# A folded self-attention product T done in three float32r passes, with new high and low parts of the sums and of the values' weights

## What is computed

```python
x = _layernorm(x + self_attention_without_softmax(x))     # (q k^T) v, 8 heads of 64, then w_o
x = _layernorm(x + cross_attention(x, ctx_1024, mask))    # softmax over 154 keys, 16 heads of 32
x = _layernorm(x + ffn(x))                                # sigmoid(x_r W_r) * (relu(x_k W_k)^2 W_v)
```

```
T   = G Wv' + s bv'            (512x512)
K'V = T' Wk' and a bias term   (only the blocks of one head count)
U   = K'V Wo',   M = Wq' U + 1,   y = x M + c
```

## Time and profile before

| | |
|---|---|
| median of 3 runs | 918.23 us (918.06 to 918.87) |
| the profiled execution | 918.05 us, of which its span, first to last instruction, is 916.3 us |
| TensorE busy | 903.6 us, 99% of the span |
| VectorE busy | 715.3 us, 78% |
| granted TensorE clock | 0.998 of full speed |

### The profile page before, as it was taken

How to read it: one execution, slowest core, us unless ns; L and a number is a source line. 1 busy time by engine, 2 the same in 40 slices (tenths; PEclk the granted TensorE clock), 3 DMA queues, 4 the chain that set the end, 5 groups by cost and what they waited for, 6 DMA issues and landing times.

```text
span 916.3 us, 19065 instructions
## 1 busy us (share of the span) xinstructions
PE 903.6 (99%) x6726; PEld 735.5 (80%) x6726; DVE 715.3 (78%) x1994; ACT 552.3 (60%) x1667; POOL 507.2 (55%) x505
## 2 busy tenths in 40 slices
PE   8999999999999999999999999999999999999997
PEld 7867767777888888887878888888787878787876
DVE  7697566577887878797979788887878787879775
ACT  7455236857765656565757575756665757575631
POOL 1053015858684757575756657575666766656420
PEclk9999999999999999999999999999999999999999
DMA  8771020113010000002000000101010100100001
GB/s 300 240 248 49 27 91 9 35 43 127 9 47 9 30 26 24 31 24 89 24 31 24 31 24 24 31 25 31 24 30 25 31 25 14 41 2 24 2 24 46
DMA packets 31033, 45.65 MB, mean 50 GB/s; under 512 B 2779, under 2 KB 15579, under 8 KB 30811
## 3 DMA queue, kind: packets, MB, share of 16 engines
q1 hardware_dynamic: 27339, 37.36, 12.7%
q10 hardware_dynamic: 3600, 7.08, 2.2%
HBM read 34.10 MB, written 9.70 MB: 48 GB/s over the span
## 4 chain that ended last, share of the span: by engine, by line
PE 75%; DVE 5%; issue 3%; POOL 3%; ACT 1%; POOLq 0%; ACTq 0%
PE dense L88 18%; PE dense L90 17%; PE dense L89 17%; PE turned L1590 5%; PE scores L1578 4%; PE rest_value L1604 4%; PE rest_value L1608 3%; PE dense L1477 2%; PE turned L1477 1%; PE rest_value L1596 1%; POOL row_inv L1383 1%; POOL prob L1389 1%; PE scores L1483 1%; DVE prob L1112 1%; DVE stats L1071 1%
## 5 line engine op out<-in xcount | busy, mean ns | idle before, releaser
L1383 POOL TENSOR_TENSOR row_inv<-row_sum,minus_one 128x4 f32<-128x4 f32 x128 | 145.9, 1139 | 255.1 <-ACT prob L794 253.5
L794 ACT ACTIVATE prob<-prob,row_min 128x154 f32<-128x154 f32 x512 | 209.5, 417 | 17.8 <-DVE row_min L1112 17.8
L1389 POOL TENSOR_TENSOR prob<-prob,row_inv 128x512 f32<-128x512 f32 x128 | 142.1, 1110 | 0.0
L1112 DVE CUSTOM_DVE_ANT_0 prob<-scores,mask_add 128x154 f32<-128x154 f32 x512 | 127.1, 310 | 3.7 <-PE scores L1578 3.7
L802 ACT ACTIVATE prob_t<-turned 128x512 f32<-128x512 f32 x128 | 75.9, 593 | 57.5 <-PE turned L1590 57.4
L794 ACT ACTIVATION_READ_ACCUMULATOR prob<-prob,row_min 128x1 f32 x512 | 98.7, 193 | 0.0
L1590 PE MATMUL turned<-ident,prob 128*128 128x128 f32 x512 | 77.0, 273 | 1.3 <-ACT prob_t L802 0.8
L88 PE MATMUL dense<-xt_hi,cross_wq_hi 128*128 128x256 f32 x256 | 75.0, 293 | 0.5 <-DVE xt_lo L1103 0.5
L88 PE MATMUL dense<-mix_k_hi,ffn_wk_hi 128*128 128x256 f32 x256 | 74.5, 291 | 0.0
L1170 DVE TENSOR_TENSOR k_act_lo<-square,k_act_hi 128x512 fp32r<-128x512 f32 x32 | 50.3, 1573 | 28.2 <-ACT k_act_hi L827 28.2
L89 PE MATMUL dense<-xt_lo,cross_wq_hi 128*128 128x256 f32 x256 | 72.2, 282 | 0.0
(11 more groups left out here) (296 smaller groups left out, 2709.4 us busy)
## 6 DMA issues: line engine op xcount, KB each, us to landing
x_rows<-x_rows SPq DMA_DIRECT2D x32, 256.0 KB, 3.6
xt_raw<-x_cols SPq DMA_DIRECT2D x16, 512.0 KB, 3.7
out<-gate_then_y SPq DMA_DIRECT2D x15, 512.0 KB, 2.8
mask_in<-mask SPq DMA_DIRECT2D x16, 154.0 KB, 2.4
cross_wv<-cross_wv SPq DMA_DIRECT2D x2, 512.0 KB, 5.9
cross_wk<-cross_wk SPq DMA_DIRECT2D x1, 1024.0 KB, 8.7
self_wv<-self_wv ACTq DMA_DIRECT2D x1, 1024.0 KB, 7.6
self_wk<-self_wk ACTq DMA_DIRECT2D x1, 1024.0 KB, 12.0
```

What stands on the lines that cost most here:

```text
L794: m = act.activation(keys, keys, ACT.Exp, bias=row_min[:, buf, t, h:h + 1], scale=-1.0, accum_out=row_sum[:, buf, t, h:h + 1])
L1112: m = dve.tensor_tensor_reduce(prob[buf][:, t, h * CTX:(h + 1) * CTX], s_bank[:, h, t * CTX:(t + 1) * CTX], mask_add[n % 2][:, t, :], -SCA ...
L1383: pool.tensor_tensor(row_inv[:, buf, t, :], row_sum[:, buf, t, :], minus_one[:], ALU.pow).then_inc(*p_inv.up)
L1389: pool.tensor_tensor(keys[:, :, 0:P], keys[:, :, 0:P], inv.broadcast_to([P, HPG, P]), ALU.mult).then_inc(*p_norm.up)
```

## The change

T of both batches is done as three float32r passes. For that:

- G of each batch gets a high part (ScalarE, `sums_high`, four operations of 128x512) and a low part (VectorE, `sums_low`, four).
- The values' weights `self_wv` get a high part (ScalarE, one operation of 128x2048) and a low part (VectorE, one). ScalarE makes the high one after `high(14, 15)` and VectorE the low one before `low(16, 17)`. `self_wv` is put elsewhere in memory, and its load is issued later: after the keys of the context are out, not before them.
- TensorE's order: T's first half now comes after tiles 20 and 21 instead of before, K'V after tiles 24 and 25, U after tile 28; the tiles of x that follow are the same in all.
- In `layers` VectorE builds `s_part` from the high part (four operations, as before from the whole) and then adds the low part's share (four more), after `weight_low("ffn_wk")`.
- At the end of the prologue the adding of 1 to M's diagonal (`add_one`) is split from the low part of M, so that `sums_low(1)` fits between.

```diff
@@ load and high part of the weights, ScalarE
-            load_square("self_wv")
-            load_row("self_bv")
             load_square("self_wk")
...
+            load_square("self_wv")
+            load_row("self_bv")
             high(12, 13)
             load_row("self_bk")
-            high(14, 15, 16, 17)
+            high(14, 15)
+            weight_high("self_wv")
+            high(16, 17)
             take_sums(0)
...
             high(20, 21)
             load_square("self_wq")
+            sums_high(0)
             high(22, 23)
+            def sums_high(b):
+                for i in range(KT):
+                    act.wait_ge(*g_whole.at(b, i + 1))
+                    act.activation(g_two[b][0][:, i, :], g[b][:, i, :], ACT.Copy).then_inc(*g_act.up)
...
                 act.activation(t[0][:, i, :], m_bank[i][:], ACT.Copy).then_inc(*m_out.up)
+                if i == 0:
+                    sums_high(1)
@@ VectorE
-            low(*range(10, 18))
+            low(*range(10, 16))
+            weight_low("self_wv")
+            low(16, 17)
             take_sums(0)
             low(18, 19)
             take_mirror(0)
             low(20, 21)
+            sums_low(0, *range(KT))
             take_columns(0)
+            def sums_low(b, *parts):
+                for i in parts:
+                    dve.wait_ge(*g_act.at(b, KT // 2 + i + 1))
+                    dve.tensor_tensor(g_two[b][1][:, i, :], g[b][:, i, :], f32(g_two[b][0][:, i, :]),
+                                      ALU.subtract).then_inc(*g_whole.up)
...
-            take_m(0)
-            take_m(1)
+            add_one(0)
+            dve.wait_ge(*xt_high.at(0))
+            dve.tensor_tensor(xt_lo[:], xt_in[:], f32(xt_hi[:]), ALU.subtract).then_inc(*xt_low.up)
+            take_m(0)
+            add_one(1)
+            sums_low(1, 0, 1)
+            take_m(1)
+            sums_low(1, 2, 3)
+            add_one(2)
@@ TensorE
-                        m = pe.matmul(t_bank[i][:], g[0][:, k, i * P:(i + 1) * P], f["self_wv"][:, k, :],
-                                      start=(k == 0), stop=(k == KT - 1))
+                        m = three_pass(pe, t_bank[i][:], [x[:, k, i * P:(i + 1) * P] for x in g_two[0]],
+                                       [x[:, k, :] for x in self_wv_two], first=(k == 0), last=(k == KT - 1))
...
             columns(0)
-            pe.wait_ge(*f_here["self_wv"].at(0))
+            sums(20, 21)
+            pe.wait_ge(*w_low.at(place_of("self_wv")))
+            pe.wait_ge(*g_whole.at(0))
             t_product(0, 1)
-            sums(20, 21)
+            sums(22, 23)
             pe.wait_ge(*s_ok.at(0))
             t_product(2, 3)
-            sums(22, 23)
+            sums(24, 25)
...
-            sums(24, 25, 26, 27)
+            sums(26, 27, 28)
...
-            sums(28, 29, 30, 31)
+            sums(29, 30, 31)
@@ layers
-            sum_weights()
+            sum_weights(0)
             take_t(0)
...
                     take_t(2)
                     weight_low("ffn_wk")
+                    sum_weights(1)
...
-                        m = pe.matmul(t1_bank[i], g1[:, k, i * P:(i + 1) * P], fold["self_wv"][:, k, :],
-                                      start=(k == 0), stop=(k == KT - 1))
+                        m = three_pass(pe, t1_bank[i], [x[:, k, i * P:(i + 1) * P] for x in g1_two],
+                                       [x[:, k, :] for x in wv_two], first=(k == 0), last=(k == KT - 1))
```

More of the change, by code:

```diff
@@ L128, in prologue @@
     u0, u0_two, wq_two = f["u"][0], f["u_two"][0], f["wq_two"]
+    g_two, self_wv_two = f["g_two"], f["wv_two"]
     gram = [banks[0:4], banks[4:8]]
@@ L137, in prologue @@
     early = ("cross_wq", "cross_wo")
-    splits = [weights[name] for name in early] + [(f["self_wq"], *wq_two)]
+    splits = {"self_wv": (f["self_wv"], *self_wv_two), **{name: weights[name] for name in early},
+              "self_wq": (f["self_wq"], *wq_two)}
+    place_of = list(splits).index
     t_bank, u_bank, m_bank = ([banks[i] for i in x] for x in ((3, 0, 1, 2), (1, 2, 3, 0), (1, 2, 3, 0)))
@@ L224, in high, with weight_high @@
                     act.activation(x_half[j % RING], by_k(x_in[j % RING]), ACT.Copy, scale=0.5).then_inc(*halved.up)
-            def weight_high(i):
-                raw, hi, _ = splits[i]
-                act.wait_ge(*(w_here[early[i]] if i < len(early) else f_here["self_wq"]).at(0))
+            def weight_high(name):
+                raw, hi, _ = splits[name]
+                act.wait_ge(*(w_here if name in early else f_here)[name].at(0))
                 act.activation(hi[:], raw[:], ACT.Copy).then_inc(*w_high.up)
@@ L273, in act_program @@
             load_square("self_wq")
+            sums_high(0)
             high(22, 23)
             load_row("self_bo")
-            for i in range(len(splits)):
-                weight_high(i)
+            for i, name in enumerate((*early, "self_wq")):
+                weight_high(name)
                 high(2 * i + 24, 2 * i + 25)
@@ L310, in low, with weight_low @@
                     dve.tensor_tensor(by_k(x_lo[i]), by_k(x_in[i]), f32(x_hi[i]), ALU.subtract).then_inc(*split_lo.up)
-            def weight_low(i):
-                raw, hi, lo = splits[i]
-                dve.wait_ge(*w_high.at(i))
+            def weight_low(name):
+                raw, hi, lo = splits[name]
+                dve.wait_ge(*w_high.at(place_of(name)))
                 dve.tensor_tensor(lo[:], raw[:], f32(hi[:]), ALU.subtract).then_inc(*w_low.up)
@@ L370, in dve_program @@
             take_t(0, 1)
-            weight_low(0)
+            weight_low("cross_wq")
             low(24, 25)
-            weight_low(1)
+            weight_low("cross_wo")
             take_t(2, 3)
             low(26, 27)
-            weight_low(2)
+            weight_low("self_wq")
+            low(28)
             dve.wait_ge(*kv_mm.at(0))
@@ L379, in dve_program @@
                 dve.tensor_copy(kv_t[0][r, q, r], kv_bank[r, c]).then_inc(*kv_ok.up)
-            low(28, 29)
-            low(30, 31)
+            low(29, 30, 31)
             def c_times(q, at):
@@ L420, in dve_program @@
             take_m(2)
+            add_one(3)
             take_m(3)
@@ L467, in mirror @@
                 pe.wait_ge(*g_dve.at(b))
-                pe.wait_ge(*g_act.at(b))
+                pe.wait_ge(*g_act.at(b, KT // 2))
                 for i in range(KT):
@@ L474, in columns @@
             def columns(b):
-                pe.wait_ge(*g_whole.at(b))
+                pe.wait_ge(*g_whole.at(b, KT))
                 pe.wait_ge(*summed.at((b + 1) * HALF - 1))
@@ L538, in pe_program @@
                 pe.matmul(u_bank[q][:], kv_t[0][:, q, :], f["self_wo"][:, q, :], start=True, stop=True).then_inc(*u_mm.up)
-            sums(28, 29, 30, 31)
+            sums(29, 30, 31)
             pe.wait_ge(*u_ok.at(0))
             pe.wait_ge(*c_part_ok.at(0, 2 + KT))
-            pe.wait_ge(*w_low.at(2))
+            pe.wait_ge(*w_low.at(place_of("self_wq")))
             m_product(0)
@@ L552, in pe_program @@
             pe.wait_ge(*m_out.at(0, 1))
+            pe.wait_ge(*g_whole.at(1))
             for k in range(KT):
-                pe.matmul(t1_bank[:], g[1][:, k, 0:P], f["self_wv"][:, k, :], start=(k == 0), stop=(k == KT - 1))
+                three_pass(pe, t1_bank[:], [x[:, k, 0:P] for x in g_two[1]], [x[:, k, :] for x in self_wv_two],
+                           first=(k == 0), last=(k == KT - 1))
         with nc.Block():
@@ L598, in layers @@
     col_sb = io["col_sb"]
-    g1, t1, kv_t1, u1 = (fold[x][1] for x in ("g", "t", "kv_t", "u"))
-    u1_two, wq_two = fold["u_two"][1], fold["wq_two"]
+    g1_two, t1, kv_t1, u1 = (fold[x][1] for x in ("g_two", "t", "kv_t", "u"))
+    u1_two, wq_two, wv_two = fold["u_two"][1], fold["wq_two"], fold["wv_two"]
     s_col, s_part, c_part = (fold[x] for x in ("s_col", "s_part", "c_part"))
@@ L1019, in take_t, with sum_weights @@
                                              ALU.mult, ALU.add).then_inc(*ft_ok.up)
-            def sum_weights():
-                dve.tensor_scalar(s_part[:], fold["self_bv"][:], float(S) / P, None, ALU.mult).then_inc(*fs_part.up)
+            def sum_weights(half):
+                if half == 0:
+                    dve.tensor_scalar(s_part[:], fold["self_bv"][:], float(S) / P, None, ALU.mult).then_inc(*fs_part.up)
                 for k in range(KT):
-                    dve.wait_ge(*fs_part.at(0, k + 1))
-                    dve.scalar_tensor_tensor(s_part[:], fold["self_wv"][:, k, :], s_col[:, 1, k:k + 1], s_part[:],
+                    dve.wait_ge(*fs_part.at(0, half * KT + k + 1))
+                    dve.scalar_tensor_tensor(s_part[:], f32(wv_two[half][:, k, :]), s_col[:, 1, k:k + 1], s_part[:],
                                              ALU.mult, ALU.add).then_inc(*fs_part.up)
@@ L1882, in decoder_layer @@
             "g": [mem.over("x1_0", "g0", square), mem.over("mix_k_hi", "g1", square)],
```

(4 more changed lines are left out.)

11 lines of the change are left out of this document (5 added, 6 removed).

## The result

The changed kernel takes **919.89 us** in the median of 15 runs (918.51 to 922.12), the kernel before 918.06 (917.61 to 918.87, 15 runs beside it): a ratio of 1.0020, 95% interval 1.0012 to 1.0028. That is a small loss at the edge of 0.2%, where 917.0 and a small gain were forecast, and outside the range.

The account below looks back on a forecast made before the run. TensorE, busy 99% of the span, was taken as the bound. -5.5 saved + 0.7 (layers' turning) + 0.7 (tile 16) + 2.9 (T) = -1.2 us, so the median 918.23 becomes 917.0 us; range 914.3 to 919.0.

Parts of the forecast that it names:

- What TensorE saves: Eight parts of T in three passes: each takes 2.74 us instead of 3.43, saving 5.5 us in all.
- What of that stands in the layers: Layers keep 1.4 us of 2.1; 0.7 becomes a wait before the turning; the prologue's end gives 0.7.
- about 0.5: Layers, before VectorE's first scores: about 0.5 us of cover left after s_part's added steps; without it up to 0.7 lost.
- Tile 16: Tile 16, ahead of T of batch 0: TensorE waits 0.7 us behind the values' weight's split; bounds 0.7 and 5.6.
- the third rival: Before tile 16: the values' weight lands after 12.0 us, TensorE waits 5.6 us, time 921.9 us; chance 0.07.
- The price of a meeting: Around T of batch 0: a GpSimd add meeting VectorE costs 1.07 us per low part, 0.9 per s_part step.
- their number: Before tile 22's low part: four GpSimd adds meet VectorE's work, the middle of three and five.
- From there to M: From tile 22's low part to M: no further loss counted, bounds 0.5 for VectorE and 0.3 at U.
- the step *T.: T of batch 0: TensorE waits 2.9 us in sum, at T's start or tile 22; bounds 1.8 and 4.0.
- VectorE's queue has no gap: Around T of batch 0: five adds are due and VectorE works without a pause in which they could run unmet.
- Rival 4: Layers' 1.4 us gain is lost too, or six adds meet at T: 918.4 us; chance 0.14 (to 919).

Follow-up runs that it names:

- batch 0 as before: Changed kernel with T of batch 0 back in float32 and its old place, self_wv split behind tile 29; 916.21 us.
- the fastest: Changed kernel with three weights' loads, self_wv's split and s_part later, T's parts 2 and 3 taken ahead of cross_wo's low part; 914.56 us.
- the fill: Changed kernel plus four float32 matmuls that compute nothing, two ahead of tile 21 and two ahead of T; 919.62 us.
- second profile: Changed kernel without further edit, measured again on another chip, median 919.97 us; the profile is of its run of 923.27 us.
- loads later: Changed kernel with the loads of cross_wo, self_wq and self_wo issued behind the high parts of tiles 20 and 21; 916.70 us.
- adds on one column: Changed kernel with GpSimd adding only one column of tiles 20 to 31 into batch 1's column sums, output wrong; 916.99 us.
- both later: Changed kernel with the three weights' loads behind tile 21's copies and self_wv's split behind tiles 16 and 17; 917.78 us.

## Why the prediction was wrong

**Right, by its steps.** *What TensorE saves*: T's second half takes 5.54 us, 74.41 to 79.95, 2.77 a part for 2.74. *What of that stands in the layers*: the turning's wait is 0.65 for 0.7. VectorE's cover before its first scores is 0.66 for "about 0.5", in its timeline:
```profile
133.74 3.11 DVE L1062 SCALAR_TENSOR_TENSOR s_part<-self_wv_lo,s_col,s_part 128x512 f32<-128x512 f32 x4
137.50 0.32 DVE L1149 CUSTOM_DVE_ANT_0 prob<-scores,mask_add 128x154 f32<-128x154 f32 x1 [0.66 <-PE scores L1616]
```
Layers and prologue's end together came out at 2.2 for 2.1, by the experiment with batch 0 as before. *Tile 16*: 0.56 by its bracket and 0.72 by its start, for 0.7; the values' weight took 5.6 us to land, for 6 to 6.5, so the third rival was out. The price of a meeting, 1.07 us, is right, and so is their number: with the tiles in time four meet, and tile 22's low part is taken at 66.67 for 66.8. *From there to M* is right as well: from tile 22 to M it is 28.63 us in the changed kernel (71.37 to 100.00) and in the fastest (64.02 to 92.65), for the 28.6 of the forecast.

**Wrong: the step *T.***, "2.9 us in sum, at T's start or at tile 22". What failed in it is the landing of tile 21. The step saw that load(20) falls behind the loads of two weights, and gave both tiles the 7.1 us of tile 22 in the kernel before: "Tiles 20 and 21 then land at 53 to 54.5". Tile 20 was there at 53.9, tile 21 at 57.6, after 9.3 us. With that its other premise fell, that "VectorE's queue has no gap": VectorE stood 2.48 us for tile 21 and TensorE 1.89, then 2.50 more at T. That is 4.4 us for 2.9, with the bound at 4.0, and the clock hides more: VectorE has the low part of tile 22 at 70.1, 3.3 later than the 66.8 of the forecast. Of these, 2.5 are the gap and 0.4 were there before tile 16; the rest is about half a meeting more. With the tiles in time the step came out as forecast.

**Left out: the clock.** It fell to 0.50 behind the wait at tile 21. The prediction counts a wait at its own length; in the profiled execution the matmuls behind it were 2.1 us slower, 1.3 of it net. In the median this is a few tenths (0.35 by the fill).

**Small: gaps ahead of tile 22.** Where VectorE is not late, the order itself has 0.5 us that the forecast lacks. The fastest kernel takes 18.1 us from tile 16 to tile 22, 0.46 of it the wait before the columns (54.44 for 53.98), where the forecast has 17.2. Of the 0.5, 0.23 is tile 18, whose low part is out at 50.79 and taken at 50.84, without a bracket. The sum of that kernel closes with both: -5.5 + 0.7 + 0.5 + 0.5 = -3.8, measured -3.7.

For the median itself, 919.9 - 917.0 = 2.9 us are to be explained. The 3.3 us by which tile 22's low part is late, less the 0.4 from before tile 16, are 2.9, all of it; the clock's few tenths come on top. These are of one execution that lies 1.7 above the median, so the books close to about 0.5 us and no better.

One sum of the prediction is off. Rival 4 puts six meetings at T at 918.4 us; by the prediction's own price they wait 62.5 + 6.4 - 63.9 = 5.0 us, 2.1 above the 2.9, and the time is 919.1, just outside its range.

Of the rivals, the one on the slow side was the wrong one: the weight that might land late was self_wv, and the load that did was a tile's.

## What to carry to other kernels

When a step is put ahead of another in an engine's queue, follow the buffer that the delayed one frees, to the load that waits for it, and ask what that load now stands behind; here tile 21's load was issued 3.7 us later than before (48.27 for 44.60), beside two weights, and took 9.3 us. Work that nobody needs soon (s_part, cross_wo's low part) belongs behind the low part that TensorE takes next: two moves on VectorE were worth 3.2 us here by the medians (917.78 to 914.56), more than the 2.8 that the change itself had in that stretch. And an edit that takes away one wait is judged only when the next one behind it is gone too: two good edits together gained nothing over either (917.78 against 916.70 and 917.05).

## What the runs showed of the hardware

- In the changed kernel the granted clock went from 1.00 to 0.50 1.3 us after a wait of 1.89 us, and stayed there for some 7 us (0.43 us from one 512-column matmul to the next, 0.23 otherwise); a second wait, of 2.50 us, came within the slow stretch. After a wait of 2.01 us it went down in the same way (second profile). Waits of 1.51 and 0.48 us (loads later) and of 1.56 and 1.15 (adds on one column) left it at 1.00, and none of those 22 runs has a mean under 0.998. With 1.55 us in the profile, five of eleven runs had a mean of 0.996 or 0.997 (both later); that this wait did it there is not shown. The Trainium skill (TensorE: Matmul & The Clock Gate, Part 1) has the gate pass half of the pulses when the engine has been little busy; the trace agrees with its 0.50.
- Matmuls that compute nothing, put into such waits, kept the clock at 1.00 and took the upper end off the runs (923.27 to 920.31), but hardly moved the median.
- A tile of 256 KB took 9.3 us from issue to use when two loads of 1 MB had been issued 1.7 and 1.0 us before it, 7.1 when 2.5 and 1.9 us before it, 4.2 without them.
